# A selective scan: the products of state and C for two states in one VectorE instruction, results in a ring of four

## The reference, cut to what matters

```
x_conv = silu(causal_conv(x_in)); B, C, dt from x_conv; dt = softplus(...)
dA  = exp(dt * A)                      # per feature d, state n, token t
dBx = dt * B * x_conv
h_t = dA_t * h_{t-1} + dBx_t           # along the 512 tokens
y_t = sum over n of h_t[d, n] * C_t[n]
out = (y * silu(z)) @ out_proj
```

## Time and profile before

| | |
|---|---|
| median of the timed executions | 1133.44 us |
| the profiled execution, its own time | 1120.12 us |
| its span, first to last instruction | 1118.3 us |
| the scan stage, first scan to last product | 719.5 to 855.6 us |
| TensorE matmul busy over the whole span | 994.4 us, 89% |
| VectorE busy | 622.1 us, 56% |
| ScalarE busy | 535.1 us, 48% |
| GpSimd busy | 199.0 us, 18% |
| mean granted TensorE clock | 0.957 |

### The profile page before, as it was taken

How to read it: one execution, slowest core, us unless ns; L and a number is a source line. 1 busy time by engine, 2 the same in 40 slices (tenths; PEclk the granted TensorE clock), 3 DMA queues, 4 the chain that set the end, 5 groups by cost and what they waited for, 6 DMA issues and landing times.

```text
span 1118.3 us, 11610 instructions
## 1 busy us (share of the span) xinstructions
PE 994.4 (89%) x3718; PEld 432.0 (39%) x3718; DVE 622.1 (56%) x1164; ACT 535.1 (48%) x978; POOL 199.0 (18%) x176
## 2 busy tenths in 40 slices
PE   5799999998799999998885996877778999999896
PEld 3345545454222232332233663322223444444343
DVE  2223232434788868767342445489997544545573
ACT  4233232223367767666741452666665324564540
POOL 9100000000000000000274660256762000000000
PEclk9799999999899999999997997989999999999998
DMA  8630000040011211210011436000000311110032
GB/s 173 196 109 0 1 1 1 8 85 0 22 56 49 63 44 50 57 31 0 7 35 48 132 90 191 11 1 0 0 1 1 104 49 47 48 38 20 11 104 75
DMA packets 67020, 54.70 MB, mean 49 GB/s; under 512 B 18584, under 2 KB 58829, under 8 KB 66868
## 3 DMA queue, kind: packets, MB, share of 16 engines
q1 hardware_dynamic: 64660, 51.26, 16.8%
q0 software_dynamic: 2304, 2.76, 0.8%
HBM read 41.65 MB, written 13.77 MB: 50 GB/s over the span
## 4 chain that ended last, share of the span: by engine, by line
PE 70%; DVE 11%; issue 7%; ACT 6%; POOL 3%; DMA 2%; SPq 1%; DVEq 0%; POOLq 0%; ACTq 0%
PE psum L694 66%; DVE sb_scr L2359 3%; ACT sb_scr L1662 3%; POOL expert_in L652 2%; DVE sb_scr L2708 2%; DVE sb_scr L2717 2%; ACT psum L1662 1%; ACT sb_qstack L1662 1%; PE psum L1273 1%; PE psum L855 1%; PE psum L1255 1%; POOL sb_scr L674 1%; DVE sb_x L2197 0%; DVE sb_scr L2221 0%; DMA sb_scr<-pick_rows 0%
## 5 line engine op out<-in xcount | busy, mean ns | idle before, releaser
L1662 ACT ACTIVATE sb_scr<-psum 128x512 f32<-128x512 f32 (+3 forms) x640 | 320.2, 536 | 347.8 <-PE psum L694 296.8
L694 PE MATMUL psum<-sb_h,sb_wide 128*128 128x512 f32 x448 | 211.1, 600 | 0.8 <-ACT sb_scr L1662 0.8
L2359 DVE TENSOR_REDUCE sb_scr<-psum 128x2 f32<-128x1024 f32 x128 | 154.9, 1223 | 46.9 <-PE psum L694 46.6
L694 PE MATMUL psum<-sb_scr,sb_wide 128*128 128x512 f32 x256 | 125.6, 594 | 0.8 <-DVE sb_scr L2763 0.8
L694 PEld LDWEIGHTS psum<-sb_h,sb_wide 128*128 128x128 f32 x448 | 83.7, 193 | 93.6 <-issue 91.9
L694 PE MATMUL psum<-sb_kstack,sb_qstack 96*128 96x512 bf16 x256 | 98.8, 397 | 8.3 <-DVE sb_scr L2359 8.2
L694 PE MATMUL psum<-sb_qstack,sb_kstack 128*128 128x512 bf16 x256 | 99.7, 396 | 3.9 <-ACT sb_scr L1662 2.8
L2285 DVE TENSOR_SCALAR sb_scr<-psum,sb_b 128x512 f32<-128x512 f32 x48 | 34.6, 748 | 117.3 <-PE psum L694 117.3
L674 POOL TENSOR_TENSOR sb_scr<-sb_scr 128x512 f32<-128x512 f32 x64 | 83.1, 1304 | 89.8 <-ACT sb_scr L1662 44.9
L1662 ACT ACTIVATE sb_scr<-psum,sb_b 128x512 f32<-128x512 f32 x48 | 31.3, 685 | 139.3 <-PE psum L694 139.3
L645 POOL COPY sb_wide<-sb_wide 128x512 f32<-128x512 f32 x4 | 2.5, 622 | 505.5 <-ACT sb_scr L1662 505.5
(11 more groups left out here) (278 smaller groups left out, 1282.6 us busy)
## 6 DMA issues: line engine op xcount, KB each, us to landing
sb_scr<-weight_rows SPq DMA_DIRECT2D x32, 256.0 KB
sb_qstack<-q_bounce SPq DMA_DIRECT2D x48, 96.0 KB
sb_kstack<-k_bounce SPq DMA_DIRECT2D x144, 32.0 KB
sb_scr<-pick_rows SPq DMA_DIRECT2D x8, 512.0 KB
expert_in<-sb_scr SPq DMA_DIRECT2D x4, 645.0 KB, 6.6
sb_scr<-expert_in SPq DMA_DIRECT2D x8, 322.5 KB
expert_out<-sb_scr SPq DMA_DIRECT2D x4, 512.0 KB, 4.9
sb_scr<-expert_out SPq DMA_DIRECT2D x8, 256.0 KB, 4.4
```

The source lines that it names most:

```text
L694: return nc.tensor.matmul(out_, w, r, start=start, stop=stop, **kw)
L1662: return nc.scalar.activation(out_, in_, func, **kw)
L2359: v.reduce_max(headmax[:, g % 2, t:t + 2, j], banks, AX.X).then_inc(sem("maxed"), 1)
```

## The change

The product of state and C is formed for two states by one VectorE instruction, which reads C's two banks and two places of the `state` ring and writes two places of `read`, a ring of four now. `read_ready` counts pairs. VectorE runs it after the scan of every even i, for states i - 2 and i - 1. On TensorE, only the even ones of spread_c and add_state wait, for the pair; and in the loop spread_b(i+5) now stands ahead of spread_c(i+2).

```diff
--- before.py
+++ after.py
@@ -289,7 +289,8 @@
         dt, dtx, zgate = (batches(NB * S * n) for n in range(3))
         RB, RC, RD = 4, 2, 2
         drive, bcast_b, state = (ring(6144 + RB * S * n, RB) for n in range(3))
-        read = ring(6144 + 3 * RB * S, 2)
+        RR = 4
+        read = ring(6144 + 3 * RB * S, RR)
 
         spare_q, spare_k = (t[:].rearrange("p h s -> p (h s)").bitcast(F32) for t in (qstack, kstack))
         dtv, dtl = (spare_q[:, NB * S * n:NB * S * (n + 1)].rearrange("p (b s) -> p b s", b=NB) for n in range(2))
@@ -1397,14 +1398,15 @@
 
             def spread_c(i):
                 b, n = divmod(i, NSTATE)
-                if i >= RC:
-
-                    pe.wait_ge(sem("read_ready"), i - RC + 1)
+                if i >= RC and i % 2 == 0:
+
+                    pe.wait_ge(sem("read_ready"), i // 2)
                 mm(bank(2 + i % RC), pick[:, NSTATE + n, :], wparts[:, b, :]).then_inc(sem("c_done"), 1)
 
             def add_state(i):
-                pe.wait_ge(sem("read_ready"), i + 1)
-                mm(bank(6), eye[:], read[:, i % 2, :], i % NSTATE == 0, i % NSTATE == NSTATE - 1).then_inc(sem("y_added"), 1)
+                if i % 2 == 0:
+                    pe.wait_ge(sem("read_ready"), i // 2 + 1)
+                mm(bank(6), eye[:], read[:, i % RR, :], i % NSTATE == 0, i % NSTATE == NSTATE - 1).then_inc(sem("y_added"), 1)
 
             def project_out(b):
 
@@ -1447,10 +1449,10 @@
                     step_size(3)
             pe.wait_ge(sem("dtv_ready"), NB + 1)
             for i in range(NSCAN):
+                if i + B_AHEAD < NSCAN:
+                    spread_b(i + B_AHEAD)
                 if i + RC < NSCAN:
                     spread_c(i + RC)
-                if i + B_AHEAD < NSCAN:
-                    spread_b(i + B_AHEAD)
                 if i % NSTATE == 0 and i >= NSTATE:
                     project_out(i // NSTATE - 1)
                 if i >= NSTATE and i % NSTATE == 5:
@@ -2704,17 +2706,19 @@
                 dve.wait_ge(sem("drive_ready"), i + 1)
                 if i >= RB:
 
-                    dve.wait_ge(sem("read_ready"), i - RB + 1)
+                    dve.wait_ge(sem("read_ready"), (i - RB) // 2 + 1)
                 v.tensor_tensor_scan(state[:, i % RB, :], bank(4 + i % RD), drive[:, i % RB, :], 0.0,
                                      ALU.mult, ALU.add).then_inc(sem("scanned"), 1)
 
-            def read_state(i):
-                dve.wait_ge(sem("c_done"), i + 1)
-                if i >= 2:
-
-                    dve.wait_ge(sem("y_added"), i - 1)
-                dve.wait_ge(sem("scanned"), i + 1)
-                v.tensor_tensor(read[:, i % 2, :], bank(2 + i % RC), state[:, i % RB, :], ALU.mult).then_inc(sem("read_ready"), 1)
+            def read_pair(i):
+
+                dve.wait_ge(sem("c_done"), i + 2)
+                if i >= RR:
+
+                    dve.wait_ge(sem("y_added"), i - RR + 2)
+                dve.wait_ge(sem("scanned"), i + 2)
+                v.tensor_tensor(read[:, i % RR:i % RR + 2, :], psum[:, 2:2 + RC, :], state[:, i % RB:i % RB + 2, :],
+                                ALU.mult).then_inc(sem("read_ready"), 1)
 
             def gate_batch(b):
                 dve.wait_ge(sem("y_added"), b * NSTATE + NSTATE)
@@ -2735,8 +2739,8 @@
                     scan(i)
                 if b >= 1 and n == 1:
                     gate_batch(b - 1)
-                if i >= 1:
-                    read_state(i - 1)
+                if i >= 2 and i % 2 == 0:
+                    read_pair(i - 2)
                 if b >= 1 and n == 4:
                     add_batch(b - 1)
                 if b >= 1 and n == 11:
```

## The result

| | before | after |
|---|---|---|
| median of the timed executions | 1133.47 us | 1187.51 us |
| ratio of the two, 95% interval | | 1.0497 (1.0457 to 1.0537) |
| the profiled execution, its own time | 1120.12 us | 1187.45 us |
| its span | 1118.3 us | 1185.6 us |
| mean granted TensorE clock over the span | 0.957 | 0.932 |

A forecast was written before the change was run, and what follows sets the result against it. The prediction took a wait loop through TensorE and ScalarE to bound the kernel. It added 36.9 us for the longer loop and 8.5 for the clock, 45.4 on 1133.44, giving 1178.8 us; 8 in 10 lay from 1164 to 1204.

The forecast's parts named there:

- The rows and the loop of before: Scan stage: a wait loop through TensorE and ScalarE takes 3.72 us per two states, 5.13 per pair after the change.
- The product over two banks: VectorE: one product over 1024 elements takes 1.22 us for two of 0.67, making VectorE's floor 3.39 us per pair.
- The larger ring: The ring for read waits on adds long done, so its larger size is worth nothing.
- Low turns: Scan-stage loops with TensorE's clock low (1.2 GHz) take 6.40 us, 1.27 more than at full clock.
- The batch's additions: In each of three batches, gate 0.54 us, projection and variance 0.87 each; together 3 x 2.28 = 6.84 us.
- the softplus of iteration 5: ScalarE, between a copy of B and the next decay: adds 1.94 us to the loop; the other two softpluses cost nothing.
- The clock: TensorE in the scan stage: low clock 28% of the time, so 24% of loops, 6.7 of 28, costing 8.5 us.
- The sum: From the product of state 3 to the last gate: 36.9 us with the start plus 8.5 for clock, 45.4 longer.
- The stage's end: After the full loops: one loop at VectorE's floor, 3.39 us, then 6.69 up to the last gate.
- full clock throughout: Rival for the scan stage: loop of 5.13 us holds and the clock does not fall, 1170.3 us; chance 0.22.
- low throughout: Rival for the scan stage: TensorE's clock low nearly throughout, 77.6 us longer, 1211.0 us; chance 0.08.
- VectorE as the bound: Rival for the scan stage: spread_b released early enough, 3.39 us per pair for 3.72, 10.2 less, 1123.2 us; chance 0.07.

The follow-up runs named there:

- e1: Changed kernel with both spread_b of a pair run ahead of the spread_c that waits for the pair: 1146.97 us, ratio 1.0152 to the kernel before.
- e4: Changed kernel with ScalarE's copies of B two states ahead of its decays instead of three: 1141.78 us, ratio 1.011 to the kernel before.
- e3: Changed kernel with spread_c(i+2) ahead of spread_b(i+5) again, the pairing without the swap: 1221.46 us, ratio 1.0792 to the kernel before.
- e7: Kernel before, single products, with a ring of four for read instead of two: 1125.15 us, ratio 0.998 to the kernel before.
- e6: Kernel before, single products, with ScalarE's copies of B two states ahead of its decays instead of three: 1119.28 us, ratio 0.9879.

## Why the prediction was right, and where its size was off

- The rows and the loop of before: right. The same arithmetic that gives 3.72 us for two states gives 5.13 for the changed order, and 5.11 was measured. Cutting the loop at TensorE (e1) or at ScalarE (e4) removed it, lengthening it by 0.44 (e3) lengthened the turns by 0.43.
- The product over two banks: 1.22 forecast, 1.200 measured; VectorE's floor 3.39, measured 3.36 in e1 and e4. The rule of the Trainium skill ("VectorE: DVE Perf Modes", Rules for kernel authors), fewer chained operations, is worth 0.06 us per pair here (3.42 to 3.36), 1.9 us in 32. The estimate from the formula in its section on the errata was 5.0.
- The larger ring at nothing: right on single products (e7, 0.998).
- Low turns at 6.40: 6.39 measured.
- The batch's additions: 0.54 for the gate, measured 5.57 - 5.11 = 0.46; 0.87 for the projection, 5.97 - 5.11 = 0.86; the variance 6.13 - 5.11 = 1.02, for the logarithm behind it costs something too, which I left out; the softplus of iteration 5 1.94, 7.04 - 5.11 = 1.93. That of iteration 8 was put at nothing; its turn took 5.43 at full clock, 0.32 more.
- The clock: this term was mis-sized, 8.5 us forecast. From the product at 739.52 to that at 911.29 are 28 turns in 171.8 us. At full clock, with the additions just named, they would be 28 x 5.11 + 3 x (0.46 + 0.86 + 1.02) + 1.93 = 152.0. So the clock took 19.8 us, or 19.5 without that third softplus. I had expected 28% of the time at the low level and 24% of the loops. It was 32% of the time (mean 0.84), which by the same translation would be 27% of the loops and 9.7 us. But the low time fell on the bursts: 16 of 28 began with a burst at less than 1.00. The step that failed is the translation of a mean over time into a share of loops.
- The sum: 56.9 us in the stage against 45.4. Of the 11.5 that were missing, the clock has 11.3. The stage's end took 10.88 (4.07 and 6.81) for 10.08, and the start and the batch's terms 0.6 less than forecast.
- The rivals: full clock throughout was wrong by its own sign, the granted 0.84, and low throughout was as wrong. The argument against it has a slip: by its own terms TensorE would be busy for 1.66 + 3.42 of 6.40 us there, 79% and not over 80%. VectorE as the bound did not come about in the changed kernel; it did in e1 and e4, where the copy's dependence on the pair was cut, and even there the expected gain of 10 us was not to be had with pairs. It was to be had with single products (e6), by 1.2%. The forecast left the batch's matmuls and the clock out of that rival, and they are what pairs lose by in e4.

## What to carry to other kernels

Before joining two instructions, ask not what their fixed part costs but who was released by the first of them: here 0.06 us per pair was saved on VectorE and 1.4 us added, since TensorE's next spread of B, ScalarE's copy and the decay behind it were released once per pair, at the pair's end. Walk round the loop of waits once with starts from the timeline and the new order; if that walk gives the old period for the old order, trust it for the new one. And where two engines in order hand work to each other, first look how far ahead each runs: one state less of copying ahead gained 1.2%, more than the change was after.

## What the runs showed of the hardware

A granted clock averaged over a stretch can understate what it costs an engine that works in bursts. A turn with 0.75 on average, 0.50 in the burst and 0.97 after it, took 6.39 us, as much as the 6.40 worked out for 0.50 throughout. And adding 87 matmuls that compute nothing made the kernel 1.3% faster, as it left only 5 bursts of 28 under full clock instead of 16.
